# Cross-attention softmax: the row maxima subtracted through a masked 64-row product instead of a diagonal matrix

## The reference

```python
# layer 0: x = x + xattn(layernorm(x), ctx);  H = 16, HD = 16
Q = x @ Wq + bq
K, V = jnp.split(text_input @ Wkv + bkv, 2, axis=-1)
scores = jnp.einsum('bqhd,bkhd->bhqk', Q, K) * scale
out = jnp.einsum('bhqk,bkhd->bqhd', jax.nn.softmax(scores, axis=-1), V)
# layer 1: x = x + xattn(layernorm(x), ctx);  H = 8, HD = 32
A = jax.nn.softmax(jnp.einsum('bqhd,bkhd->bhqk', qh, kh) / np.sqrt(DIM_V), axis=-1)
O = _layernorm((qh + jnp.einsum('bhqk,bkhd->bqhd', A, vh)).reshape(B, NQ, DIM_V), g0, b0)
O = _layernorm(O + jax.nn.relu(O @ Wo.T + bo), g1, b1)
```

## Time and profile before

| | us |
|---|---|
| median of 3 runs | 2270.12 (2255.2 to 2271.07) |
| the profiled execution | 2271.3 |
| its span | 2268.6 |
| PE busy | 1862.0 (82%) |
| DVE busy | 1394.0 (61%) |
| POOL busy | 987.0 (44%) |
| ACT busy | 799.5 (35%) |

### The profile page before, as it was taken

One profiled execution on the slowest core, in us unless ns is written; L12 is line 12 of the kernel. 1 busy time (PEld: TensorE's weight loads), 2 busy tenths in 40 slices (PEclk: granted clock), 3 DMA queues, 4 the chain that ended last, 5 costly groups with the idle time before them and its releaser, 6 DMA issues. The chain is left out here.

```text
span 2268.6 us, 44822 instructions
## 1 busy us (share of the span) xinstructions
PE 1862.0 (82%) x14222; PEld 1319.0 (58%) x14223; DVE 1394.0 (61%) x2612; ACT 799.5 (35%) x1535; POOL 987.0 (44%) x1128
## 2 busy tenths in 40 slices
PE   6988888888888749999698888888887268888884
PEld 4656565665566426666477777777775135555552
DVE  5877777777778442222277777777776624444442
ACT  3545445444454302222254444444442011111110
POOL 4444444444444201111355555555553026666663
PEclk8999989899899769999799999999997579999998
DMA  4111111100000041111202121111110232222223
GB/s 108 37 45 35 46 51 35 37 23 17 25 17 13 9 181 33 32 32 32 71 22 69 47 66 50 42 48 30 30 31 8 80 89 38 38 38 37 37 39 79
DMA packets 54161, 102.05 MB, mean 45 GB/s; under 512 B 11842, under 2 KB 37674, under 8 KB 50698
## 3 DMA queue, kind: packets, MB, share of 16 engines
q1 hardware_dynamic: 37754, 78.87, 10.9%
q0 software_dynamic: 16352, 22.47, 5.4%
HBM read 79.78 MB, written 24.93 MB: 46 GB/s over the span
## 5 line engine op out<-in xcount | busy, mean ns | idle before, releaser
L825 DVE TENSOR_REDUCE a_mx<-a_SM 100x2 f32<-100x722 f32 x384 | 348.6, 908 | 90.8 <-PE a_SM L406 74.4
L1424 PE MATMUL e_PH<-w,e_xT 128*128 x712 | 327.5, 603 | 6.0 <-DVE e_ab L1556 2.9
L666 POOL TENSOR_TENSOR a_rstd<-a_ve,a_half_neg 100x1 f32<-100x1 f32 x224 | 129.6, 579 | 393.4 <-DVE a_ve L784 393.4
L629 ACT ACTIVATE a_Pr<-a_ST 120x800 f32<-120x800 f32 (+1 forms) x288 | 241.6, 839 | 160.9 <-PE a_ST L433 160.9
L406 PE MATMUL a_SM<-a_KTb,a_QMb 64*100 64x361 bf16 x768 | 141.1, 364 | 131.3 <-DVE a_mx L825 125.8
L711 POOL TENSOR_TENSOR a_DM<-a_neg_ident,a_mx 100x800 bf16<-100x800 bf16 x96 | 147.7, 1538 | 166.3 <-DVE a_mx L825 166.3
L1424 PEld LDWEIGHTS e_PH<-w,e_xT 128*128 128x128 f32 x712 | 135.2, 194 | 142.0 <-issue 139.1
L444 PE MATMUL a_M<-a_Pr,a_V 120*32 120x100 f32 (+3 forms) x4608 | 202.4, 279 | 0.3 <-ACT a_Pr L629 0.3
L1345 POOL COPY e_gidx<-toks 128x1 int32 (+1 forms) x89 | 48.4, 544 | 300.5 <-PE e_PX L1413 205.7
L406 PEld LDWEIGHTS a_SM<-a_KTb,a_QMb 64*100 64x100 bf16 x768 | 48.2, 122 | 217.0 <-DVE a_mx L825 172.4
L444 PEld LDWEIGHTS a_M<-a_Pr,a_V 120*32 120x32 f32 (+3 forms) x4608 | 156.5, 133 | 24.0 <-issue 15.7
(11 more groups left out here) (186 smaller groups left out, 4299.5 us busy)
## 6 DMA issues: line engine op xcount, KB each, us to landing
w<-in_E_w SPq DMA_DIRECT2D x24, 1024.0 KB, 5.0
a_ct<-in_ctx SPq DMA_DIRECT2D x64, 362.0 KB, 3.1
keep_rows<-a_keep SPq DMA_DIRECT2D x64, 100.0 KB
tile_rows<-e_y SPq DMA_DIRECT2D x32, 128.0 KB
b_rows<-in_E_b SPq DMA_DIRECT2D x1, 4096.0 KB
sums<-X SPq DMA_DIRECT2D x1, 3200.0 KB
out<-sums SPq DMA_DIRECT2D x2, 1600.0 KB, 9.4
X<-in_x SPq DMA_DIRECT2D x1, 2800.0 KB
```

The costliest lines, as they stand in the source:

```text
L629: nc.scalar.activation(dst.rearrange("p (j q) -> p j q", j=2), ST[0:n, (b.p * NS + s) % 2, :, 0:4 * LQ], ACT.Exp, scale=SCALE).then_inc(ex ...
L666: nc.gpsimd.tensor_tensor(rstd[k][:], ve[k][:], half_neg[:], ALU.pow).then_inc(rstd_ready[k], 1)
L825: V_.tensor_reduce(pair, SM[0:LQ, :, 0:LK], AX_X, ALU.max).then_inc(max_done, 1)
L1424: last = nc.tensor.matmul(PH[:, h, :], xT[:, c, :], rhs, start=(c == 0), stop=(c == DC - 1))
```

## The change

The diagonal matrices go. At the end of a step DVE copies each maximum into as many columns as its head has in the 256-wide layout (`repeat_max`, two copies into `mxr`). At the start of the next step, ahead of `front`, PE multiplies the two halves of `mxr` by a negative identity, which transposes them (`max_columns`); ACT copies the result to `mxT`; POOL multiplies it by the head mask (`masked_max`, `MXM`), eight heads at a time. In each slot the two products of ones now have 64 rows, in the two halves of the array as L433 has, with `MXM` as the other operand. The negative identity is divided by the head's width, since each maximum now stands in that many rows.

```diff
-        DM = sb("DM", [LQ, H, LQ], BF16)
+        mxr = sb("mxr", [LQ, DC, 128], BF16)
+        mxT = sb("mxT", [128, DC, LQ], BF16)
+        MXM = sb("MXM", [128, DC, HT, LQ], BF16)
...
+            def max_columns(b):
+
+                pe.wait_ge(mxr_ready, b.count(1, 1))
+                for c in range(DC):
+                    last = nc.tensor.matmul(ST[:, 1, 0, c * LQ:(c + 1) * LQ], mxr[:, c, :], neg_ident[:],
+                                            start=True, stop=True)
+                last.then_inc(mxT_ps, 1)
...
                 if kt == 0:
-                    pe.wait_ge(dm_ready, b.count(EIGHTS, eight + 1))
+                    pe.wait_ge(mxm_ready, b.count(EIGHTS, eight + 1))
...
-                    h = 8 * eight + 4 * j
-                    nc.tensor.matmul(ST[0:n, buf, j, 0:4 * LQ], ones_bf[:, 0:n], DM[:, h:h + 4, :],
-                                     start=True, stop=False)
+                    rows = place(8 * eight + 4 * j)[0]
+                    nc.tensor.matmul(ST[0:n, buf, j, 0:4 * LQ], ones_bf[rows, 0:n],
+                                     MXM[rows, C * eight:C * eight + C, :, :], start=True, stop=False)
...
             def step(b, fr, ahead, back, tail):
                 nxt, nxt2, prev = b.plus(1), b.plus(2), b.plus(-1)
+                if back:
+                    max_columns(b)
                 if fr:
                     front(nxt)
...
+            def max_columns(b):
+                act.wait_ge(mxT_ps, b.count(1, 1))
+                act.wait_ge(mxm_ready, b.count(EIGHTS))
+                nc.scalar.activation(mxT[:], ST[:, 1, 0, 0:DC * LQ].rearrange("p (c q) -> p c q", c=DC), ACT.Copy
+                                     ).then_inc(mxT_ready, 1)
...
-            def diagonals(b, e):
-
-                pool.wait_ge(max_done, b.count(NP, 4 * e + 4))
+            def masked_max(b, e):
+
+                pool.wait_ge(mxT_ready, b.count(1, 1))
                 if b.low >= 1:
                     pool.wait_ge(st_ps, b.count(NS, 3 * e + 3 - NS))
...
+                if back:
+                    for e in range(EIGHTS):
+                        masked_max(b, e)
                 if fr:
                     low_parts(nxt)
...
                 if fr and layer == 0:
                     masked_low(nxt, 0)
-                    diagonals(nxt, 0)
...
                     masked_low(nxt, EIGHTS - 1)
-                    diagonals(nxt, EIGHTS - 1)
...
+            def repeat_max(b):
+
+                dve.wait_ge(max_done, b.count(NP, NP))
+                dve.wait_ge(mxT_ps, b.count(1))
...
+                    last = V_.tensor_copy(out, heads.unsqueeze(len(heads.shape)).to_broadcast(list(out.shape)))
+                last.then_inc(mxr_ready, 1)
...
+                if fr:
+                    repeat_max(nxt)
                 if back:
                     normalise(b)
```

More of the change, by code:

```diff
@@ L162, in attention @@
         neg_ident = sb("neg_ident", [LQ, LQ], BF16)
-        ones_bf = sb("ones_bf", [LQ, 128], BF16)
+        ones_bf = sb("ones_bf", [128, 128], BF16)
         mask = sb("mask", [128, HT])
+        mask_bf = sb("mask_bf", [128, HT], BF16)
         half_neg = sb("half_neg", [LQ, 1])
@@ L252, in attention @@
         max_done = sem("max_done")
-        dm_ready = sem("dm_ready")
+        mxr_ready = sem("mxr_ready")
+        mxT_ps = sem("mxT_ps")
+        mxT_ready = sem("mxT_ready")
+        mxm_ready = sem("mxm_ready")
         st_ps = sem("st_ps")
@@ L704, in masked_low @@
                     mask[:].unsqueeze(1).unsqueeze(3).to_broadcast([128, C, HT, LQ]), ALU.mult).then_inc(ql_ready, 1)
-            def diagonals(b, e):
-                pool.wait_ge(max_done, b.count(NP, 4 * e + 4))
+            def masked_max(b, e):
+                pool.wait_ge(mxT_ready, b.count(1, 1))
                 if b.low >= 1:
                     pool.wait_ge(st_ps, b.count(NS, 3 * e + 3 - NS))
-                nc.gpsimd.tensor_tensor(DM[:, 8 * e:8 * e + 8, :], neg_ident[:].unsqueeze(1).to_broadcast([LQ, 8, LQ]),
-                                        mx[:, 8 * e:8 * e + 8].unsqueeze(2).to_broadcast([LQ, 8, LQ]), ALU.mult
-                                        ).then_inc(dm_ready, 1)
+                C = DC // EIGHTS
+                nc.gpsimd.tensor_tensor(
+                    MXM[:, C * e:C * e + C],
+                    mxT[:, C * e:C * e + C, :].unsqueeze(2).to_broadcast([128, C, HT, LQ]),
+                    mask_bf[:].unsqueeze(1).unsqueeze(3).to_broadcast([128, C, HT, LQ]), ALU.mult).then_inc(mxm_ready, 1)
             def residual1(b):
@@ L758, in _ @@
                 nc.gpsimd.memset(V[p][:, :, :, HD:HD + 1], 1.0)
-            nc.gpsimd.tensor_scalar(neg_ident[:], ident[0:LQ, 0:LQ], -1.0, 0.0, ALU.mult, ALU.add
+            nc.gpsimd.tensor_copy(mask_bf[:], mask[:])
+            nc.gpsimd.tensor_scalar(neg_ident[:], ident[0:LQ, 0:LQ], -1.0 / HD, 0.0, ALU.mult, ALU.add
                                     ).then_inc(pads_set, 1)
@@ L821, in maxima @@
                 if j == 0:
-                    dve.wait_ge(dm_ready, b.count(EIGHTS))
+                    dve.wait_ge(mxr_ready, b.count(1))
                 dve.wait_ge(sm_ps, b.count(NP, j + 1))
@@ L826, in maxima @@
                                  ).then_inc(max_done, 1)
+            def repeat_max(b):
+                dve.wait_ge(max_done, b.count(NP, NP))
+                dve.wait_ge(mxT_ps, b.count(1))
+                for c in range(DC):
+                    if layer == 0:
+                        heads = mx[:, 8 * c:8 * c + 8]
+                    else:
+                        heads = mx[:].rearrange("q (j c m) -> q c j m", j=2, c=DC)[:, c]
+                    out = mxr[:, c, :].rearrange("q (h r) -> q h r", r=HD)
+                    if layer == 1:
+                        out = mxr[:, c, :].rearrange("q (j m r) -> q j m r", j=2, r=HD)
+                    last = V_.tensor_copy(out, heads.unsqueeze(len(heads.shape)).to_broadcast(list(out.shape)))
+                last.then_inc(mxr_ready, 1)
             def normalise(b):
```

3 lines of the change are left out of this document (2 added, 1 removed).

## The result

The changed kernel takes **2305.11 us**, median of 4 runs (2303.0 to 2308.45), beside 2270.6 us for four runs of the kernel before on the same chip. The ratio is 1.017, its 95% interval 1.014 to 1.020. The profiled execution took 2304.6 us (span 2302.7), 33.3 more than the profiled one of before.

What follows compares the result with a forecast made beforehand. Neither engine alone was taken as the bound: PE and DVE hand a chain to and fro once a step, with POOL's order on layer 1's path. 2271.3 + 92 (layer 1) + 9 (layer 0) gave 2372 us, range 2310 to 2450.

Steps and rivals of the forecast that it cites:

- Slots (1): PE's slots: each 0.2 to 0.3 us shorter; in layer 0 PE only waits longer, so counted as 0.
- Diagonals off POOL (2): DVE sums no longer beside POOL's DM: -1.15 us a step in layer 0, -0.9 us in layer 1.
- The opposite case that was left out: Layer 1: the new masked product holds off one DVE operation; sum up to 25 us higher, not counted.
- Head (3): Step's start: PE waits for last reduction and two copies; front later, +1.2 us in layer 0, +1.65 in layer 1.
- POOL's queue and what is late next (4, 5): Layer 1: masked_max behind power(2, prev) and gather, PE waits 2.35 us, scores(b, 0) +4.0 us; +2.0 left after old waits.
- The clock (6): PE's clock: one fall to half speed every layer 1 step, +1.9 us; layer 0 adds 0.25 us a step.
- Layer 1's term: Layer 1's whole addition: +3.05 us a step over 30 steps, 92 us; range 1.8 to 4.0 a step.
- Layer 0's +0.3: Layer 0's whole addition: +0.3 us a step over 31 steps, 9 us; range -0.5 to +1.2 a step.
- B: Rival: POOL reaches masked_max before 1360.75, queue hidden, only the head counts; about 2307 us, chance 0.09.
- A: Rival: PE's clock falls much more, two falls each layer 1 step (24.3 us); 2450 us, chance 0.13.
- C: Rival: not slower; DVE's list, freed of POOL's products, pulls the step; 2227 us or near 2270, chance 0.08.

Runs made afterwards that it cites:

- mxm_first_inside: Changed kernel with layer 1's masked_max ahead of power(2, prev) and the gather, and both layers' transposing products and ACT's copy inside front: 2216.95 us, ratio 0.977.
- pool_kept_busy: Changed kernel plus an extra, unread POOL product of the old diagonals' size in the middle of layer 0's step: 2329.32 us (one run).
- mxm_first: Changed kernel with layer 1's masked_max moved on POOL ahead of power(2, prev) and the gather: 2277.03 us, ratio 1.005.
- inside_only: Changed kernel with the transposing products and ACT's copy inside front, masked_max left behind the gather: 2306.11 us, ratio 1.016.
- new_layer0: Kernel before with the change in layer 0 only, layer 1 built by the old function: 2268.51 us, ratio 1.001.
- head_wait_timed: Kernel before plus a PE wait for the last maximum at each step's head, ahead of front, both layers: 2251.43 us, ratio 0.9945.
- front_wait: Kernel before plus a PE wait in layer 1, behind front and ahead of scores(b, 0), for the next queries: 2297.04 us, ratio 1.013.
- gather_late: mxm_first_inside with layer 1's gather moved on POOL to right behind power(1, prev): 2256.0 us, ratio 0.996 to the kernel before.
- dm_late: Kernel before with layer 1's diagonals moved on POOL behind the gather, nothing else: 2396.01 us (one run).

## Why the prediction missed, step by step

**Slots (1): under-sized.** 0.41 us a slot, not 0.2 to 0.3. In layer 0 the earlier arrival did go into a longer wait, as "I count 0" has it: the second pair's wait went from 0.9 to 1.6 us. In most steps of the changed kernel the clock falls behind it, but that this wait brings the fall is not shown: mxm_first_inside has the same wait (1.57) in a step without one.

**Diagonals off POOL (2): right.** 1.33 us off the sum in layer 0 (1.15 forecast), confirmed by pool_kept_busy. The opposite case that was left out, a DVE operation beside the masked product, exists: the text took statistics and a reduction to stand there, but with the head later it is the sum L896, 1.00 us where it takes 0.42 before. DVE has slack behind it, since its next reduction waits 2.8 us for PE; but `MXM` itself takes 1.07 us there and 0.85 in mxm_first, and PE waits for `MXM`. No run tried it apart.

**Head (3): mechanism right, size high.** 0.45 us behind the reduction to the products and 0.10 for these, 0.55 where 0.9 was forecast; the wait for `mxr` is 1.36 us in layer 1 (about 1.3 forecast) and 0.83 in the step of layer 0 shown. In layer 1 the forecast lets POOL's queue set the start of `scores(b, 0)`, whatever the head takes, and inside_only bears this out: 20.57 us with the head and without it. In layer 0 the times cancel as forecast (new_layer0: 1.001), and mxm_first_inside is 1.04 a step faster than before. That is partly luck: the falls of the clock cost more than before, since the time at half speed rose from 4.3 to 6.7 us a step, and the slots, counted at nothing, are among what can have made up for it; no run takes these apart. One small slip: two copies of 0.15 or 0.6 us each would move the sum to -0.15 or +0.75, not -0.3 or +0.7.

**POOL's queue and what is late next (4, 5): right almost to the number.** `MXM` stands behind the gather, PE waits 2.33 us (2.35 forecast), the wait of the third pair shrinks, and 2.07 us are left at full clock (2.0 forecast). Some of this closeness is luck, since errors cancel: `power` starts 3.4 us behind the last reduction's start, not 3.7, and `MXM` takes 1.07 us, not 0.85. mxm_first takes the queue away and gets 1.13 of the 2.07.

**The clock (6) is the step that failed.** It said: "I take one fall in every step, and a little more than 1.45 for it", +1.9, so that a step would take 22.4 us. The falls nearly vanished, from 17 of 24 steps to 4: a step takes 20.79 us at a clock of 0.99, and the falls cost 0.22 us a step where 1.9 was set. Layer 1's term is 1.27 us a step, not 3.05; 30 x 2.07 = 62 us less 30 x 0.80 = 24 given back is 38, and 41.6 was measured from the first to the last step. "With the clock as now it would be +2.0" stood there and would have given 2340, still too high. The error was to count idle time: more waits, so more falls. The runs do not bear that out. In layer 1, by 24 steps each:

```
kernel            PE's longest waits, us                      waits, us a step  falls in  clock  us a step
before            1.6 to 2.2 at the third pair                2.1               17 of 24  0.93   19.52
head_wait_timed   1.0 at the head, 0.8 to 1.3 at the third    2.5                3 of 24  0.99   18.97
changed           1.4 at the head, 2.3 behind front           5.1                4 of 24  0.99   20.79
mxm_first         1.4 at the head, 1.5 at the second          3.6               11 of 24  0.94   20.03
mxm_first_inside  1.6 to 2.0 at the third                     2.2               16 of 24  0.91   19.34
front_wait        1.7 to 2.7 behind front                     2.8               20 of 24  0.91   20.71
inside_only       3.1 to 3.3 behind front                     4.7               23 of 24  0.90   22.29
gather_late       1.0 to 1.4 at the second, to 2.3 at affs    3.5               24 of 24  0.92   20.56
dm_late           4.2 behind front                            4.7               24 of 24  0.86   23.90
```

The changed kernel has PE idle for longest and has almost no falls, so the sum of the idle time does not decide. Nor does one wait's place or length alone: waits behind `front` stand in rows with few and with many falls. One thing does go along with the falls: the three kernels in which PE waits about 1 us or more at the head of a step are the three with fewest, and in head_wait_timed this wait is all that was added. It is no rule either, since in layer 0 the changed kernel has that wait too (0.4 to 0.8 us), and there PE is at half speed for longer than before. What exactly decides stays open.

**Layer 0's +0.3** was +0.01 a step in the 20 steps. What is left at the layers' ends is -12.9 us, which the forecast did not have; 8.5 of it shows in the old code too.

**The rivals.** B's 2307 is close to the time, but its mechanism, the queue hidden, did not occur: PE waits for `MXM` in each step. A's steps of 24 us came only in dm_late; in the changed kernel PE's idle time grew from 2.1 to 5.1 us a step of layer 1 and the falls went from 17 to 4 steps. C's freed DVE list was real, and needed the head out of the way: 2217 in mxm_first_inside.

## What to carry to other kernels

Price a change at full clock first, from steps at full clock, and put the clock in as a term of its own with both signs: here one added wait took falls away (head_wait_timed) and another brought them (front_wait), and the sum of PE's idle time did not tell which. When an operation takes the place of another on a queue of an engine, look at what stands ahead of it there, and what then runs beside its neighbours. Two delays that lie side by side are not worth the sum of both. Here one operation moved ahead of a gather, and two products moved into cover, made a loss of 1.7% a gain of 2.3%.

## What the runs showed of the hardware

- PE's granted clock fell to half in 17 of 24 steps of the kernel before, whose longest wait of PE there is 2.2 us; with one wait of 1.0 us more at the head of a step it fell in 3 of 24 (granted clock 0.99 for 0.93, time 0.9945), and with one of 1.7 to 2.7 us behind `front` in 20 of 24 (time 1.013).
- From a pair of bf16 products of 64 rows and 400 columns to the second 64-row pair behind it is 0.35 us; with a pair of 100 rows in its place it is 0.76.
- A DVE sum of two SBUF operands took 411 ns with no product of POOL beside it and 1735 to 1741 beside POOL's 100x800 product; another took 0.42 us in the kernel before and 2.65 in mxm_first, beside POOL's 128x722 product. The Trainium skill, SBUF — State Buffer, section "Who interferes with whom", has it that a DVE instruction with two SBUF inputs contends with a GpSimd one that reads SBUF. These runs agree with it.
- From the start of `power` to the end of the gather's issue POOL needs 2.93 us (1390.71 to 1393.64 in the timeline above; 3.05 before), of which 0.91 are idle: the gather with its index copy is a long entry on POOL's queue.
